# A wavelet convolution followed by a median filter: the last two images taken whole, early products for other images, and five output sums given to GpSimd

## The reference, cut to what matters

```python
# layer 0: a Haar wavelet transform, a 1x1 convolution with batch norm and ReLU on each band,
# the inverse transform, beside it x itself (three levels down and up again), then a 3x3 convolution
cA, cH, cV, cD = dwt2(x)
proc = lambda c: batchnorm_relu(jnp.einsum('bchw,oc->bohw', c, conv_w), bn_gamma, bn_beta)
rimg0 = idwt2(proc(cA), proc(cH), proc(cV), proc(cD))
rimg1 = ...                        # perfect reconstruction: x
rimg = jnp.concatenate([rimg0, rimg1], axis=1)
y = conv3x3(rimg, convW_w) + convW_b
x = batchnorm_relu(y, bnW_gamma, bnW_beta)      # statistics over all 16 images
# layer 1: a 3x3 median, a 1x1 convolution, and the input added
x_denoised = median_blur(x, 3)
return x + jnp.einsum('bchw,oc->bohw', x_denoised, W) + b[None, :, None, None]
```

## Time and profile before

| | |
|---|---|
| median of 3 runs | 406.03 us |
| the profiled execution | 405.87 us, span 403.6 us |
| granted clock of PE | 0.998 of full speed |
| PE busy | 391.7 us (97% of the span) |
| DVE busy | 372.1 us (92%) |
| POOL busy | 216.7 us (54%) |
| ACT busy | 168.5 us (42%) |

### The profile page before, as it was taken

The page is one execution under the profiler, slowest core; times in us unless marked ns, Lnnn a source line. Parts: engine busy times, 40 slices in busy tenths (PEclk is TensorE's granted clock), DMA queues, the critical chain, the costliest instruction groups (busy, mean ns, idle before and its releaser), DMA issues.

```text
span 403.6 us, 3844 instructions
## 1 busy us (share of the span) xinstructions
PE 391.7 (97%) x1202; PEld 223.1 (55%) x1202; DVE 372.1 (92%) x528; ACT 168.5 (42%) x364; POOL 216.7 (54%) x208
## 2 busy tenths in 40 slices
PE   7889999999999999999999999999999999998996
PEld 2334568877544445454545555554546588853432
DVE  3799956999949999999999999999999999999996
ACT  1456756322334624243333333434324322266762
POOL 3999469454633548475664747584743440023332
PEclk9999999999999999999999999999999999999999
DMA  8980010010101010101101010101010100003547
GB/s 298 415 353 2 2 52 1 2 52 0 54 1 52 1 52 2 52 0 52 30 24 52 1 54 1 52 1 52 2 52 9 43 2 1 2 0 132 232 168 300
DMA packets 7794, 26.70 MB, mean 66 GB/s; under 512 B 992, under 2 KB 1248, under 8 KB 7776
## 3 DMA queue, kind: packets, MB, share of 16 engines
q1 hardware_dynamic: 7776, 26.48, 17.3%
HBM read 18.09 MB, written 8.39 MB: 66 GB/s over the span
## 4 chain that ended last, share of the span: by engine, by line
PE 61%; DVE 29%; issue 4%; ACT 3%; POOL 1%; DMA 1%; DVEq 0%; SPq 0%; POOLq 0%; ACTq 0%
PE conv_ps L422 43%; PE conv_ps L437 10%; PE one_ps L404 4%; DVE y L996 3%; PE one_ps L515 2%; PE conv_ps L539 2%; DVE sorted_cols L870 1%; DVE sorted_cols L872 1%; DVE sorted_cols L865 1%; DVE sorted_cols L910 1%; DVE one_ps L920 1%; DVE sorted_cols L916 1%; DVE one_ps L899 1%; DVE z L901 1%; DVE z L742 1%
## 5 line engine op out<-in xcount | busy, mean ns | idle before, releaser
L422 PE MATMUL conv_ps<-ru,wt 128*128 128x512 f32 (+1 forms) x360 | 131.1, 500 | 0.0
L422 PEld LDWEIGHTS conv_ps<-ru,wt 128*128 128x128 f32 x360 | 68.2, 190 | 49.5 <-issue 45.7
L422 PE MATMUL conv_ps<-xu,wt 128*128 128x496 f32 (+3 forms) x240 | 87.4, 500 | 0.0
L652 ACT ACTIVATE y<-conv_ps,sgn 128x512 f32<-128x512 f32 (+1 forms) x40 | 25.5, 638 | 129.9 <-PE conv_ps L422 129.9
L422 PEld LDWEIGHTS conv_ps<-xu,wt 128*128 128x128 f32 x240 | 45.5, 190 | 31.7 <-issue 28.6
L251 POOL TENSOR_TENSOR ru<-z 128x512 f32<-128x512 f32 x14 | 18.1, 1292 | 59.1 <-DVE one_ps L905 59.1
L422 PE MATMUL conv_ps<-ru,v 128*128 128x496 f32 (+3 forms) x120 | 43.8, 500 | 0.5 <-POOL ru L252 0.5
L344 POOL TENSOR_TENSOR ru<-eo 128x512 f32<-128x512 f32 x16 | 17.0, 1062 | 43.7 <-DVE one_ps L863 43.5
L404 PE MATMUL one_ps<-y,w 128*128 128x512 f32 x64 | 31.9, 636 | 4.2 <-DVE z L743 2.4
L609 ACT ACTIVATE z<-z,bn 128x256 f32<-128x256 f32 x64 | 33.0, 590 | 0.4 <-DVE bn L808 0.4
L539 PE MATMUL conv_ps<-z,w 128*128 128x512 f32 x64 | 29.5, 599 | 1.9 <-DVE y L996 1.9
(11 more groups left out here) (141 smaller groups left out, 747.1 us busy)
## 6 DMA issues: line engine op xcount, KB each, us to landing
z<-x SPq DMA_DIRECT2D x16, 512.0 KB, 10.3
raw_place<-x SPq DMA_DIRECT2D x15, 512.0 KB, 3.3
out<-y SPq DMA_DIRECT2D x15, 512.0 KB, 2.6
wt<-w_t SPq DMA_DIRECT2D x2, 576.0 KB, 10.1
ru<-x SPq DMA_DIRECT2D x1, 512.0 KB, 14.0
out<-y SPq DMA_DIRECT2D x2, 256.0 KB, 2.6
w<-w_t SPq DMA_DIRECT2D x2, 64.0 KB, 8.0
vec<-vectors SPq DMA_DIRECT2D x1, 3.0 KB, 8.9
```

Source lines behind the costliest of these rows:

```text
L422: return nc.tensor.matmul(bank(u, b)[:, (r0 - row) * BW:(r1 - row) * BW], taps(half, kx, ky), plane[:, (r0 + dy) * BW:(r1 + dy) * BW], sta ...
L652: S.activation(at(slot(n), row * W + b, [[2, cols]]), src, ACT.Identity, scale=sgn[:, :], accum_out=y_sum[:, part:part + 1]).then_inc(y_ke ...
```

## The change

Six things are changed.

1. `HALVED` loses images 14 and 15, so that there are 18 units instead of 20; the last four half units become two whole ones. Their seeds are placed as those of the images before (`LATE`), where the old kernel had a rule of its own.
2. `SPLIT` is now images 4 to 15 (12 images, images 14 and 15 among them) instead of 2, 3 and 6 to 13 (10 images). `PRE` is images 2 and 3 instead of 4 and 5. Where image 2 or 3 follows a half unit in the same bank, a small matmul of zeros fills the rest of the bank (`fill_bank`, four in all).
3. `FILLS` starts at image 6 instead of 10: 10 of the 12 early products stand between the `through_w1` calls instead of 6. The mixing of the taps is moved ahead of image 6 with it (POOL after image 5 instead of 9, ACT after image 5), and the loads of the taps come after image 5 and after image 9 instead of both after image 7.
4. `SUMMED` is (1, 3, 7, 9, 12) instead of (2, 5, 8, 11). For these images PE no longer multiplies x1 by a unit matrix; ACT copies the mixed image into `z`, and POOL adds the two (`tensor_tensor` on 1024 columns) once the image three further on is under way.
5. `BN3_AT` is 11 instead of 9, counted in images 14 and 15 (whole) instead of the last three half pieces; `FINISH_AT` is (15, 17, ... 29) instead of (16, 20, ... 44).
6. The last image is normalised, cleared and mixed by halves, as the first one.

```diff
-    FILLS = {n: 1 for n in range(10, 16)}
-    PRE = (4, 5)
-    SPLIT = (2, 3) + tuple(range(6, 14))
+    FILLS = {n: 1 for n in range(6, 16)}
+    PRE = (2, 3)
+    SPLIT = tuple(range(4, IMAGES))
...
-    SUMMED = (2, 5, 8, 11)
+    SUMMED = (1, 3, 7, 9, 12)
-    BN3_AT, FINISH_AT = 9, (16, 20, 24, 28, 32, 36, 40, 44)
-    HALVED = (0, 1, IMAGES - 2, IMAGES - 1)
+    BN3_AT, FINISH_AT = 11, (15, 17, 19, 21, 23, 25, 27, 29)
+    HALVED = (0, 1)
...
-                if n == 7:
+                if n == 5:
                     sp.dma_start(vec[:, :], vectors).then_inc(vec_in, 16)
-                    for half in (X_HALF, R_HALF):
-                        cols = slice(half * KY * KX * CH, (half + 1) * KY * KX * CH)
-                        sp.dma_start(wt[:, cols], w3_cols[:, cols]).then_inc(w3_in[half], 16)
+                if n in (5, 9):
+                    half = X_HALF if n == 5 else R_HALF
+                    cols = slice(half * KY * KX * CH, (half + 1) * KY * KX * CH)
+                    sp.dma_start(wt[:, cols], w3_cols[:, cols]).then_inc(w3_in[half], 16)
...
-                if n == 9:
+                if n == min(FILLS) - 1:
                     mix_taps(X_HALF, 1).then_inc(x_taps_mixed, 1)
...
-            for n in range(1, IMAGES):
+            for n in range(1, IMAGES - 1):
                 pool.wait_ge(med_normed, n)
                 G.memset(at(zslot(n), 0, [[(H - 1) * W, 2], [W - 1, 2]]), 0.0).then_inc(med_ready, 1)
                 if n in OWN:
                     map_x1(n)
+                if n - 3 in SUMMED:
+                    pool.wait_ge(x1_by_act, SUMMED.index(n - 3) + 1)
+                    pool.wait_ge(mix_kept, SUMMED.index(n - 3) + 1)
+                    G.tensor_tensor(slot(n - 3), slot(n - 3), zslot(n - 3), ALU.add).then_inc(out_by_pool, 1)
+            map_x1(IMAGES - 1)
+            if IMAGES - 4 in SUMMED:
...
+            corners_of_halves(IMAGES - 1, 3)
...
+            def fill_bank(u, b):
+                rest = slice(UNITS[u][2] * BW, BANK)
+                nc.tensor.matmul(bank(u, b)[:, rest], zeros[:, :], at(zeros[:, :], 0, [[0, (BANK - UNITS[u][2] * BW) // CH], [1, CH]]),
+                                 start=False, stop=False, skip_group_check=True)
...
-                    mm = nc.tensor.matmul(conv_ps[:, k, half], w2[:, :], zslot(n)[:, half], start=True, stop=n in OWN)
-                    if n in SUMMED:
-                        pe.wait_ge(x1_by_act, SUMMED.index(n) + 1)
-                        mm = nc.tensor.matmul(conv_ps[:, k, half], unit[:, :], slot(n)[:, half], start=False, stop=True)
+                    mm = nc.tensor.matmul(conv_ps[:, k, half], w2[:, :], zslot(n)[:, half], start=True, stop=True)
...
-                    S.activation(slot(n - 2), conv_ps[:, n % 2, :], ACT.Identity, bias=cb2).then_inc(out_by_act, 1)
+                    S.activation(zslot(n - 2), conv_ps[:, n % 2, :], ACT.Identity, bias=cb2).then_inc(mix_kept, 1)
...
-            last = len(UNITS) - 1
-            del EARLY[last - 3], EARLY[last - 2]
-            LATE[last - 4], EARLY[last - 3] = last - 1, last
...
-            medians(PIECES[:-3])
+            medians(PIECES[:-2])
```

48 lines of the change are left out of this document (24 added, 24 removed).

## The result

The changed kernel takes 401.84 us, the median of six executions from 400.55 to 403.58 us; the kernel before takes 405.53 us (six, 404.66 to 406.16). The ratio is 0.991, 95% interval 0.989 to 0.993. Measured again on another occasion it was 401.42 us against 405.62, ratio 0.990 [0.988, 0.992]. The forecast was 401.4.

What follows compares the result with a forecast made beforehand. PE was taken to bound until 355.6 us, DVE after 359.5. PE ends at 351.9, DVE resumes at 356.7, last median 392.0, DVE's end 396.0, transfer 399.1, plus 2.3 outside: 401.4 us, range 398.6 to 404.6.

Steps and rivals of the forecast that it cites:

- First stage: Before the units: two early products left behind image 15, 1.69 us less, 0.35 lost; unit 0 outputs at 59.15 us.
- The delay of image 6: First stage: POOL's mixing of the taps, barely ahead of PE, may make image 6 come 0.1 to 0.3 us late.
- PE's sum: Steady stage: PE's work of 291.8 us, plus 0.4 for zero products and 0.5 for small waits, ending at 351.9 us.
- wait of 5.3 us at image 2: Steady stage: DVE's 5.3 us idle time at image 2 in the old kernel was to go, with small waits from image 5.
- wait of PE for `ru12`: Steady stage: PE's 0.48 us wait for POOL does not come back; one in images 2 to 5 would be wrong.
- The last median: Last stage: DVE ends its last median 35.3 us after resuming at 356.7, at 392.0 against 394.6 before.
- the collisions: Last stage: POOL's additions and mappings block DVE instructions with two SBUF operands, 2.0 us in all (bounds 0 and 4).
- Behind the median: After the last median: 4.0 us instead of 5.9, from one addition less (1.2) and halves starting PE 0.6 us earlier.
- PE's missing 16 unit products: Last stage: PE's unit-matrix products, now dropped, said to gain nothing themselves because PE was waiting there.
- signs of being wrong: PE waits for `ru12` or put-back banks, zero products over 0.4 us each, or last-stage DVE waits over 1 us.
- the rival of less gain: Early products push image 15's bands (1 us) and collisions reach 3.5 us: 403.6 us; chance 0.21.
- POOL as the bound: No-change rival: POOL's 27 us in the last stage stretch to 38 by waits of five additions: 405.9 us; chance 0.06.

Runs made afterwards that it cites:

- experiment 3: Changed kernel with one part undone each: `FILLS` from 10, 402.78 us; `PRE` = (4, 5), 403.24 us; images 14 and 15 halved and not rounded, 408.24 us.

## Why the prediction was right, point by point

*First stage.* Forecast outputs of unit 0 at 59.15, measured 58.91 and 59.02. The cost of the moved products was named as a band of -0.1 to 1.7 and taken as 0.35, so that they give 1.35; undoing that part gives 1.26 us at the zero products. The delay of image 6 was under-sized (1.46 us idle, forecast 0.1 to 0.3), and it cost nothing, since DVE's pace had set the next images: with 1.46 in one profile of the changed kernel and 0.28 in the other, image 15 stands at 40.76 and 40.87.

*PE's sum.* Forecast 292.7 us from there to the zero products, measured 291.79, with no wait at all. The 0.5 us set aside for small waits was not needed. The prediction's sum for the kernel before fell 1.2 us short and named 0.48 of it; the rest was there too. Around its waits for ACT (65.95) and for POOL (152.35) PE lost 0.5 and 0.7 us, as in experiment 3, and both waits are gone. An image of `PRE` was 0.14 cheaper each, and the zero products cost 0.11 each (65.25, next instruction at 65.36), as taken from the earlier trace rows. Zero products of L561 at 350.70 and 350.81, forecast 351.9.

*DVE.* No wait of 5.3 us at image 2, and no wait of PE for `ru12` as in the earlier trace rows: both as said. Its first small wait came at image 7 (207.10, 0.25 us), not at 5 or 6; it caught up a little later than worked out and nothing hung on it. First median 64.88 (forecast 64.7), batch norm 353.19 (354.3), resumed 355.56 (356.7). The 1.1 us by which PE was earlier than forecast arrived whole.

*The last median.* Forecast 35.3 us after resuming, measured 36.3 and 36.2 (ends at 391.83 and 391.88). The term that was off is the collisions: 2.0 forecast, and over 0.69 us of the form L906, L908 and L916 lost 0.32, 0.97 and 1.74, together 3.0. Both collisions that the prediction named, image 3 on L908 and image 7 on L916, are the ones that happened. The Trainium skill (SBUF — State Buffer, "Who interferes with whom") has them exclude each other for the whole instruction. The traces agree: instructions of 0.39 us took 2.56 beside an addition of 2.50 us. They also decide a point that the prediction left at 2.4: POOL's addition takes 2.36 us alone, 2.79 when it meets DVE.

*Behind the median.* Forecast 4.0 us, measured 4.1 at full clock, and 6.4 when the clock had fallen. The prediction said that PE's missing 16 unit products "are worth nothing themselves, for PE was waiting there". That step failed on both sides. With unit products for all five sums PE's longest idle time is 0.96 us; without them and without additions it is 1.47; with the additions it is 1.91, since POOL's corners come later. In half of the executions the clock then falls, and these took 0.6 to 2.5 us more than the middle of the others. That is the difference between the two groups of times that the median lies between. One of the prediction's own signs of being wrong came with it: DVE waited 1.54 us for the last products in the profile with the fallen clock (0.27 at full clock). And with five sums by PE DVE would have waited for it (2.8 us), which no step of the prediction shows.

So the total was right for partly offsetting reasons: PE 1.1 us earlier than forecast; 0.9 us more up to the last median; then 0.1 or 2.4 more behind it. That the median of the six came within 0.4 us of the forecast is in part luck, for three were at full clock (400.55 to 401.04) and three were not (402.64 to 403.58), and the forecast knew of one kind only. Of the twelve executions nine lie in its 400.3 to 402.7 us, three above it, where the rival of less gain stands but not for its reasons, and none below. None reached the 405.9 of POOL as the bound: POOL is idle for over 2 us ahead of three of its corners in the profile at full clock.

What the gain consists of, in the profiles at full clock: the zero products behind the last unit start 4.8 us earlier (355.62 to 350.81), and the three parts undone one by one moved them by 1.26 (early products), 1.1 and a late start (`PRE`) and 2.3 (images 14 and 15). DVE resumes only 3.8 us earlier (359.48 to 355.66), for the batch norm starts 2.5 us behind PE instead of 1.5, as forecast: about half of that is the whole last unit, kept 1.8 us after PE's end instead of 1.3, and half the place `BN3_AT`, which DVE reached 0.7 us after the squares were summed instead of 0.2. The last stage gives 0.8 (41.09 to 40.30): up to the last median it is 1.1 longer, with collisions 1.4 dearer than the 1.6 of waits and blocks before, and behind it 1.8 shorter, with one whole addition less (1.2). At full clock POOL's additions gave 0.2 less than PE's sums would have.

**Open.** Why kernels of an equal first stage start their units between 58.5 and 59.7 us (first product at 5.84 to 6.86 us, and not in the same order) was not traced; it limits comparisons by the medians to half a microsecond or so. What else than the clock spreads the executions of one kernel, as 401.26 to 403.36 us with 12 zero products, is open too. Whether an addition of POOL placed by a wait on DVE, behind L916, would keep all of the 1.9 us was not tried.

## What to carry to other kernels

Moving work to an idle engine is priced by what it blocks, not by its own busy time: lay its instructions beside those of the bound engine that use the same port, and count the overlap. Here, with the same five additions, DVE's instructions were stretched by 3.0 us in all at one set of places and by 7.5 at another, and giving only the colliding ones back did better in that stretch than all or none. Before taking work off an engine that "waits anyway", ask whether its activity holds something up, here its clock, and work out its whole sum before adding to it.

## What the runs showed of the hardware

In five profiles PE's clock fell to its lower level (0.50 to 0.59 in a window of 4 us) at products behind idle times of 1.9 to 4.8 us, and twelve products took 7.4 to 7.8 instead of 5.57 us. By the mean clock of the runs (under 0.997) that befell 12 of 24 executions of the kernels whose longest idle time is 1.9 us, five of six with 2.6 us, all 13 with 3.6 and 4.8 us, and 4 of 51 of the kernel before with 0.78 us, where no trace shows the place. In the 4.8 us gap 16 products on zeros (3.6 us) kept it at 0.998 or more in five of six. A DVE instruction of 0.39 us with two SBUF operands took 2.56 us beside POOL's addition, and POOL's own instructions were stretched in the same stage, the addition from 2.36 to 2.79 us and the mapping from 1.20 to 1.60 (1.77 in the kernel with two of the sums by PE).
